# Moving band loads to the sync queue, storing k once and re-timing a planned macaron block on one core

## The reference

```
x = x + 0.5 * ffn(layernorm(x))        # 8 experts, summed: (silu(x @ wg) * (x @ wu)) @ wd, 128 -> 512 -> 128
x = x + attention(layernorm(x))        # 16 heads of 8 features, causal, with rotary positions
x = x + 0.5 * ffn(layernorm(x))        # the same weights
```

## Time and profile before

| | us |
|---|---|
| median of 3 runs | 1333.13 |
| lowest, highest | 1331.54, 1337.11 |
| the profiled execution | 1328.16 |
| its span, first to last instruction | 1326.4 |
| PE busy | 1307.4 |
| DVE, ACT, POOL busy | 1212.7, 1062.8, 1061.4 |

### The profile page before, as it was taken

One profiled execution on the slowest core, in us unless ns is written; L12 is line 12 of the kernel. 1 busy time (PEld: TensorE's weight loads), 2 busy tenths in 40 slices (PEclk: granted clock), 3 DMA queues, 4 the chain that ended last, 5 costly groups with the idle time before them and its releaser, 6 DMA issues. The chain is left out here.

```text
span 1326.4 us, 28468 instructions
## 1 busy us (share of the span) xinstructions
PE 1307.4 (99%) x8334; PEld 1051.4 (79%) x8334; DVE 1212.7 (91%) x2611; ACT 1062.8 (80%) x2099; POOL 1061.4 (80%) x979
## 2 busy tenths in 40 slices
PE   8999999999999999999999999999999999999998
PEld 6888888787778787778888778887888778888787
DVE  6887999999999999999999999999999999998665
ACT  6866888878888888888888888887888888887565
POOL 7976888879878887797787878788778887878565
PEclk9999999999999999999999999999999999999999
DMA  6503899999999999999999999999999999997100
GB/s 190 163 1 118 160 217 228 201 224 229 215 222 215 199 197 194 243 196 202 200 209 208 216 206 200 197 227 205 198 206 198 206 219 206 204 188 138 23 5 8
DMA packets 718555, 241.39 MB, mean 182 GB/s; under 512 B 652480, under 2 KB 681920, under 8 KB 718400
## 3 DMA queue, kind: packets, MB, share of 16 engines
q1 hardware_dynamic: 562240, 180.84, 68.0%
q10 hardware_dynamic: 156160, 58.74, 22.4%
HBM read 77.33 MB, written 69.86 MB: 111 GB/s over the span
## 5 line engine op out<-in xcount | busy, mean ns | idle before, releaser
L1247 POOL TENSOR_TENSOR hid_lo<-hid,hid_hi 128x512 fp32r<-128x512 f32 x511 | 658.8, 1297 | 174.2 <-ACT hid_hi L948 92.7
L942 ACT ACTIVATE hid<-work 128x512 f32<-128x512 f32 x512 | 306.2, 600 | 100.9 <-PE work L798 72.0
L948 ACT CAST hid_hi<-hid 128x512 fp32r<-128x512 f32 x512 | 316.2, 625 | 88.2 <-PE acc L814 55.4
L1073 DVE SCALAR_TENSOR_TENSOR hid<-hid,work 128x512 f32<-128x512 f32 x512 | 343.9, 679 | 44.3 <-ACT hid L942 43.7
L1079 DVE TENSOR_TENSOR hid<-hid,work 128x512 f32<-128x512 f32 x512 | 346.3, 680 | 23.8 <-PE work L732 20.5
L1262 POOL TENSOR_TENSOR probs<-exps,probs 128x512 f16<-128x512 f32 (+1 forms) x288 | 304.1, 1061 | 62.0 <-ACT probs L1004 58.9
L1181 DVE TENSOR_REDUCE negmax<-work 128x1 f32<-128x384 f32 (+3 forms) x352 | 219.5, 632 | 0.5
L993 ACT ACTIVATE exps<-work,negmax_shifted 128x512 f32<-128x512 f32 (+2 forms) x320 | 187.6, 601 | 37.6 <-DVE negmax_shifted L1187 27.1
L821 PE MATMUL acc<-hid_lo,wd 128*128 128x512 f32 x512 | 207.2, 409 | 1.2 <-POOL hid_lo L1247 1.1
L730 PE MATMUL work<-xt,wu 128*128 128x512 f32 x512 | 205.1, 401 | 3.0 <-DVE rope L1163 1.3
L813 PE MATMUL acc<-hid_hi,wd 128*128 128x512 f32 x512 | 203.0, 396 | 1.5 <-ACT xn L959 0.7
(11 more groups left out here) (100 smaller groups left out, 1735.0 us busy)
## 6 DMA issues: line engine op xcount, KB each, us to landing
rel_win<-rel_window_scratch ACTq DMA_DIRECT2D x128, 320.0 KB, 3.8
prob_window_scratch<-probs SPq DMA_DIRECT2D x384, 80.0 KB, 3.2
q_scratch<-rope SPq DMA_DIRECT2D x16, 512.0 KB, 4.0
qq<-q_scratch ACTq DMA_DIRECT2D x32, 256.0 KB, 3.6
k_scratch<-rope SPq DMA_DIRECT2D x16, 512.0 KB, 4.8
rel_window_scratch<-g_s SPq DMA_DIRECT2D x32, 256.0 KB, 3.3
k_pad<-k_scratch SPq DMA_DIRECT2D x128, 64.0 KB, 3.5
prob_window_scratch<-probs SPq DMA_DIRECT2D x32, 256.0 KB, 4.0
```

The costliest lines, as they stand in the source:

```text
L942: act.activation(hid[:, arg % HB, :], work[bank_of["gate", arg]][:, :], ACT.Tanh, scale=0.5).then_inc(s_tanh, 1)
L948: act.copy(hid_hi[:, arg % HH, :], hid[:, arg % HB, :]).then_inc(s_hhi, 1)
L1073: dve.scalar_tensor_tensor(out=hid[:, arg % HB, :], in0=hid[:, arg % HB, :], scalar=1.0, in1=work[bank_of["gate", arg]][:, :], op0=ALU.add ...
L1247: pool.tensor_tensor(hid_lo[:, arg % HH, :], hid[:, arg % HB, :], hid_hi[:, arg % HH, :].bitcast(F32), ALU.subtract).then_inc(s_hlo, 1)
```

## The change

Four edits. (1) `LATER` has a number for each tile of queries for the steps of a task and for the loads of windows and bands, and all its numbers are others. (2) `load_band` is a step of SP. (3) k's scratch holds each of its two parts once, and `load_k` reads each row twice by a stride of 0; the rows of q and k are ordered by head and then by feature, so the host's weights and tables are laid out accordingly, and each store moves one part of 128 rows: four stores for q, two for k. (4) Of the first norm ACT scales tiles 0 and 1, DVE tiles 2 and 3, and PE transposes 0, 2, 1, 3.

```diff
-    LATER = {"acc": -978.2, "attention_sum": -208.7, "band_turn": -699.6, "band_values": -929.8, "constants":
+    LATER = {"acc": -771.6, "attention_sum": -130.6, "band_turn": -648.8, "band_values": -988.2, "constants":
...
+    OF_TASK = ("scores", "near", "largest", "shift", "exp", "p_hi", "p_lo", "p_lent", "p_turn", "store_band")
+    def group_of(name, arg):
+        if name in OF_TASK:
+            return name + str(TASKS[arg % NK][1])
+        if name in ("load_window", "load_band"):
+            return name + str(arg % NT)
+        return name
...
-            step("SP", 1.3, at, "qk_store", (t, i), ("qk_lo", (t, i)),
+            step("SP", (2.0, 1.0)[i], at, "qk_store", (t, i), ("qk_lo", (t, i)),
...
-                step("ACT", 0.4, due[last_of(last)] + 5, "load_band", len(BANDS) * gg + u, ("store_band", last_of(last)),
+                step("SP", 0.5, due[last_of(last)] + 5, "load_band", len(BANDS) * gg + u, ("store_band", last_of(last)),
...
-    k_h = nc.dram_tensor("k_scratch", [VB * 4 * P * L], F32, kind="Internal")
+    k_h = nc.dram_tensor("k_scratch", [VB * 2 * P * L], F32, kind="Internal")
...
-                    base = t % VB * 4 * P * L
-                    for copy in range(2):
-                        sp.dma_start(bass.AP((q_t, k_t)[i], base + copy * (1 + i) * P * L,
-                                             [[L, P], [(2 - i) * P * L, 2], [1, L]]),
-                                     rope[:, :, :]).then_inc(s_qst[i], 16)
+                    places = 4 - 2 * i
+                    for place in range(places):
+                        sp.dma_start(bass.AP((q_t, k_t)[i], t % VB * places * P * L + place * H * L,
+                                             [[L, H], [places * H * L, DH], [1, L]]),
+                                     rope[:, place % 2, :]).then_inc(s_qst[i], 16)
...
-                                     bass.AP(k_t, t % VB * 4 * P * L + g * L + a * HG * L,
-                                             [[H * L, 4 * DH], [1, L]])).then_inc(s_kld[arg % 2], 16)
+                                     bass.AP(k_t, t % VB * 2 * P * L + g * L + a * HG * L,
+                                             [[H * L, 2 * DH], [0, 2], [1, L]])).then_inc(s_kld[arg % 2], 16)
+                if name == "load_band":
+                    gg, tiles = arg // len(BANDS), BANDS[arg % len(BANDS)]
+                    top, n = NT * gg + tiles[0], len(tiles)
+                    for k in range(first_of(top), last_of(NT * gg + tiles[-1]) + 1):
+                        sp.wait_ge(*stored(k))
+                    wait(sp, s_bt, 16 * gg)
+                    sp.dma_start(bands[:, tiles[0]:tiles[-1] + 1, :, :, :].rearrange("p i h a r -> p (i h a) r"),
...
-            norm_turned(0, work[2])
+            for n, i in enumerate((0, 2, 1, 3)):
+                pe.wait_ge(*((s_xn, 2 * (i + 1)) if i < 2 else (s_xn_first, i - 1)))
+                done = pe.transpose(work[2][:, i * P:(i + 1) * P], xn[:, i * P:(i + 1) * P], ident[:, :])
+            done.then_inc(s_xnt, 1)
...
-            norm_scaled(0, x_s[0], 0)
+            act.wait_ge(s_shift, 1)
+            for i in range(2):
+                act.activation(xn[:, i * P:(i + 1) * P], x_s[0][:, i * P:(i + 1) * P], ACT.Identity,
+                               scale=rstd[:, i:i + 1], bias=shift[:, i:i + 1]).then_inc(s_xn, 2)
...
-                if name == "load_band":
...
             norm_stats(0, x_s[0])
+            dve.wait_ge(s_shift, 1)
+            for i in range(2, NT):
+                dve.tensor_scalar(xn[:, i * P:(i + 1) * P], x_s[0][:, i * P:(i + 1) * P], rstd[:, i:i + 1],
+                                  shift[:, i:i + 1], ALU.mult, ALU.add).then_inc(s_xn_first, 1)
             norm_lo(0, xt[0], work[2])
```

More of the change, by code:

```diff
@@ new lines, in macaron_kernel @@
+    LATER = {"acc": -771.6, "attention_sum": -130.6, "band_turn": -648.8, "band_values": -988.2, "constants":
[3 rows of a table added]
+             1058.6, "ln_scaled": 26.7, "ln_stats": -1429.2, "ln_turned": -216.7, "lo": -320.2, "load_band0": -1084.5,
[5 rows of a table added]
+             86.1, "prepare_hi": -186.9, "prepare_lo": -372.5, "product": -34.2, "project": -162.4, "project_v": 52.5,
+             "qk_hi": -1105.5, "qk_lo": -783.5, "qk_store": -730.9, "qrel": -58.3, "qrel_copy": -319.3, "qrel_store":
[3 rows of a table added]
+             "store_band3": -349.9, "sum": 605.0, "sum_turned": -704.8, "tanh": -294.5, "up": 31.7, "v_add": 296.5,
+             "v_split": 343.5, "values": -458.6, "zero": 1447.8}
@@ L127, in step @@
             before = [(name, (arg[0], arg[1] - 1) if arg[1] else (arg[0] - 1, PARTS[name] - 1))]
-        steps[name, arg] = (engine, takes, LANDS[engine] if lands is None else lands, time + LATER.get(name, 0.0),
+        steps[name, arg] = (engine, takes, LANDS[engine] if lands is None else lands, time + LATER.get(group_of(name, arg), 0.0),
                             [what for what in after if what[1] is not None],
@@ L492, in macaron_kernel @@
         s_xn = sem("xn_of_tile_ready")
+        s_xn_first = sem("xn_of_first_norm_ready")
         s_xnt = sem("xn_transposed")
@@ L1008, in _ @@
                     t, g = arg // HG, arg % HG
-                    act.wait_ge(s_qst[0], 32 * (t + 1))
+                    act.wait_ge(s_qst[0], 64 * (t + 1))
                     if arg >= 2:
@@ L1143, in _ @@
                     if w == 2:
-                        dve.wait_ge(s_qst[0], 32 * (t + 1))
+                        dve.wait_ge(s_qst[0], 64 * (t + 1))
                     if w == 0:
@@ L1291, with by_heads @@
     f32 = np.float32
-    def dh_major(w):
-        return np.asarray(w).reshape(H, DH, P).transpose(1, 0, 2)
+    def by_heads(w):
+        return np.asarray(w).reshape(H * DH, P)
     def swapped(w):
-        return dh_major(w).reshape(DH // 2, 2, H, P)[:, ::-1].reshape(DH, H, P)
+        return by_heads(w).reshape(H * DH // 2, 2, P)[:, ::-1]
     watt = np.stack([np.asarray(m).reshape(P, P).T for m in (
-        dh_major(inputs["L0_attn_w_q"]), swapped(inputs["L0_attn_w_q"]),
-        dh_major(inputs["L0_attn_w_k"]), swapped(inputs["L0_attn_w_k"]), inputs["L0_attn_w_v"])], axis=1)
+        by_heads(inputs["L0_attn_w_q"]), swapped(inputs["L0_attn_w_q"]),
+        by_heads(inputs["L0_attn_w_k"]), swapped(inputs["L0_attn_w_k"]), inputs["L0_attn_w_v"])], axis=1)
     rel_g, rel_g0 = np.zeros((HQ, 4, DH, R, HQ), rel.dtype), np.zeros((HQ, 4, DH, R, HQ), rel.dtype)
@@ L1321 @@
     window = np.repeat(np.where(w > i + R, 1e30, 0.0), HQ, axis=1)
-    lanes = np.repeat([[0.0, 1.0], [1.0, -1.0], [0.0, 1.0], [1.0, -1.0]], DH * HQ, axis=0)
+    lanes = np.tile(np.repeat([[0.0, 1.0], [1.0, -1.0]], 2 * HQ, axis=0), (DH, 1))
     arrays = {
@@ L1326 @@
         "watt": watt.reshape(P, -1), "wo": wo.reshape(P, -1),
-        "rel_g": rel_g.transpose(1, 2, 0, 3, 4).reshape(P, P),
-        "rel_g0": rel_g0.transpose(1, 2, 0, 3, 4).reshape(P, P),
+        "rel_g": rel_g.transpose(2, 1, 0, 3, 4).reshape(P, P),
+        "rel_g0": rel_g0.transpose(2, 1, 0, 3, 4).reshape(P, P),
         "rel_c": rel_c.reshape(P, -1), "rel_c0": rel_c0.reshape(P, -1),
-        "rel_k0": np.repeat(rel[0], H)[:, None], "rel_v0": np.tile(rel[0], (P, H)),
-        "cos": np.repeat(cos, H, axis=0).astype(f32), "sin": np.repeat(sin, H, axis=0).astype(f32),
+        "rel_k0": np.tile(rel[0], H)[:, None], "rel_v0": np.tile(rel[0], (P, H)),
+        "cos": np.tile(cos, (H, 1)).astype(f32), "sin": np.tile(sin, (H, 1)).astype(f32),
         "window": window.astype(f32), "ident": np.eye(P, dtype=f32), "lanes": lanes.astype(f32),
```

2 lines of the change are left out of this document (added), and 11 rows, old and new, of the table LATER.

## The result

The changed kernel takes 1382.97 us (median of 4 runs, 1381.12 to 1384.32), the kernel before, run beside it, 1335.12 us (4 runs, 1331.54 to 1338.03). The ratio is 1.0373, 95% interval 1.0351 to 1.0395: 3.7% slower, some 48 us. The forecast of 1331, its range of 1325 to 1341 and its verdict of "no change" were all wrong.

What follows compares the result with a forecast made beforehand. TensorE, busy 1307.4 of 1326.4 us, was taken as the bound. Start -0.65, tail -0.4, ACT's relief -1 and k once -0.3 summed to -2.3 us off the 1333.13 median: 1331 us, range 1325 to 1341.

Steps and rivals of the forecast that it cites:

- load_band to SP: 128 band-load issues, 50 us, move from ACT's queue to SP's; SP's lateness counted as 0, bounds 0 to +18 us.
- The sign that I had named: In SP's queue: its waits for POOL's lower halves were to get smaller by some 50 us.
- my 4 to 16: TensorE's idle time in the middle, forecast 8 to 11 us; outside 4 to 16 us the prediction called itself wrong.
- half-speed stretch: Matmuls from 10.97 to about 14 us, 0.43 us apart, at 1.2 GHz: counted 0, bounds -1.6 to 0, far end +1.6.
- Rival B: SP becomes late in the attention stretch, TensorE waits at `values` and `band_values`: 1350 us, or 1341 in half the groups; chance 0.17.
- Arbitration between queue rows: Band loads in SP's row stand behind transposes: landing perhaps 0.2 us later, 4.9 us at the slowest transpose landing.
- Rival B's other sign: Larger DMA landing times, named beside TensorE waits in tens for turned probabilities or bands; no size given.
- ACT's relief: Band-load issues leaving ACT's queue end some of TensorE's waits for ACT: -1 us, bounds -3 to 0.
- The start: First norm scaled by ACT and DVE: first 512-column matmul near 8.7, not 9.39 us; -0.65 us, bounds -0.8 to 0.
- The tail: A down moves ahead of the program's last `up`, so two TensorE waits should go: -0.4 us, bounds -0.6 to +0.4.
- k once: k stored once: 4 MB less DMA traffic, 16 more issues on SP; together -0.3 us, bounds -1.5 to +1.
- due times: New order of gate, up, down and tasks: value 0; floor all 10.34 us of the middle gone, ceiling the same again.

Runs made afterwards that it cites:

- the kernels with 86%: Includes the kernel before with each DMA transpose replaced by two plain copies and band loads issued by SP: SP issuing 86% of 1050 us, time 1353.6 us.
- the stand-ins: Kernels with each DMA transpose replaced by plain copies (two in the main pair), the reciprocal by a multiplication: kernel before 1328.09 us, changed kernel 1359.2 us.

## Why the prediction was wrong, point by point

- **load_band to SP, the step that failed.** "so on the average there is room", and then "I count 0, bounds 0 to +18". The room was there, and more than I saw: one wait row gave 2.2 us a group, while SP's queue issues 862 of 1050 us, some 188 us free. But an average says nothing of a queue in order whose work comes in bursts (four k loads in 2.48 us, single issues of nearly 4) and whose consumers are at most four tasks behind. At 82%, in the kernel before, the bursts were absorbed; in the kernels with 86% they were not. By the stand-ins this edit costs +25.5 us in the kernel before and +39 in the changed one. The sign that I had named came: SP's waits for POOL's lower halves fell from 142.2 to 91.4 us (three lines each, 150 to 1200 us), by the 50 us forecast. I took that for room used up harmlessly, and it wasn't. TensorE's idle time in the middle became 50.6 us, far outside my 4 to 16.
- **The duration was taken from a queue with gaps.** 0.39 us is the row of ACT, where most band loads stand alone; in SP's stream, right behind other issues, the same load takes 0.52. 50 us were 67.
- **The number of those who wait was too small.** I let transposes feed `values` alone and named the buffers in half a sentence without a price. ACT's casts lost 51.1 us more than before (63.9 - 12.8), and behind them stand all other work of ACT, DVE's and TensorE's. Of TensorE's idle time 24.1 us is the direct wait; that much of the rest came this way round is argued from these waits and shown whole for one stall.
- **The clock was left out.** I had priced the half-speed stretch at the start only. New idle times brought six more: an estimated 10 of the 12.6 us by which TensorE's busy time grew.
- **Rival B** had the mechanism (SP late, waits at `values`, 0.17), but its price was the wait of before, 0.57 us, times 32 groups, +18. Measured is a mean of 24.1 / 16 = 1.5 us and up to 5.9 for the direct wait alone. A wait that the old trace shows is one in a queue that keeps up; it can't price a queue that doesn't. The sign of lateness that I quoted, transposes that took 3.9 us to issue, should have weighed more.
- **Arbitration between queue rows.** The Trainium skill (DMA: Bandwidth & Descriptors, "Queues, rings and completion order") says that each DMA engine takes turns between the queue rows. From that I had worked out that band loads would land later behind transposes. The trace doesn't show it: 3.3 us in the median from SP, 3.8 from ACT; only the longest grew, 5.8 to 8.8.
- **Rival B's other sign,** larger landing times, didn't come in the medians either.
- **ACT's relief, -1:** nothing shows it. A gain of that size can't be seen inside the loss, and the kernel before with its band loads on SP had the same relief of ACT and was 25.5 us slower.
- **The start, -0.65:** wrong. The first matmul on 512 columns stands at 9.70, not near 8.7. It starts 2.92 us behind the first scaling (6.78 to 9.70), before 2.79 (6.60 to 9.39). The rows of the changed kernel:

```profile
6.78 1.62 DVE L1092 TENSOR_SCALAR xn<-x,rstd,shift 128x128 f32<-128x128 f32 x2 [1.78 <-POOL shift L1263]
6.88 0.87 ACT L963 ACTIVATE xn<-x,shift,rstd 128x128 f32<-128x128 f32 x2
7.05 1.27 POOL L1253 TENSOR_TENSOR wg<-probs_t,wg 128x512 fp32r<-128x512 f32 x1 [0.30 <-ACT wg L949]
...
8.97 0.59 ACT L967 CAST xt<-work 128x512 fp32r<-128x512 f32 x1 [0.71 <-PE work L807]
...
9.70 0.77 PE L823 MATMUL work<-xt,wg 128*128 128x512 f32 x1 [0.77 <-POOL wu L1253]
```

DVE's two tiles took 1.62 us together, not 2 x 0.22 nor 2 x 0.41: its instruction of 128x128 was 0.35 us once and 1.36 the other time, while POOL worked beside it. The last transpose waited for it, and ACT's gain was lost. In three stand-ins with the same edit the two took 1.52 to 1.55 us. The same step alone was worth nothing in its run.
- **The half-speed stretch, 0:** right. Matmuls still start 0.43 us apart behind the first one, until 12.8 us. The clock column has 1.00 there, so it is the spacing that tells it, not the column.
- **The tail, -0.4:** the two waits of the earlier trace rows are gone; the kernel's last stage idles 3.64 us where 3.75 were, so right in kind and, in total, nearly nothing.
- **k once, -0.3, and due times, 0:** right within what can be told when each is alone (+0.4 and +0.2 us as stand-ins). Yet the order isn't indifferent: two plans of the same work, issued by the same engines, lay 17 us apart, and the three parts together cost 9 us that none costs alone. A sum of single steps can't see this.
- **Still open:** the stand-ins show 31 of 48 us. Issues of over 2 us are frequent only in the originals (from 150 to 1200 us 42 transposes in each, 110 us together in each; in the stand-ins five issues at most); that a queue with such issues is hurt more by added ones is likely but was not shown.

## What to carry to other kernels

An engine that only issues DMAs is a resource like any other: sum its issues over a stretch before giving it more, with durations of issues that stand as closely as the new ones will. Don't measure its room by an average, but ask how many tasks ahead of their consumers the buffers let it be, and what is the longest run of issues in a row. And follow the buffers backwards: the first to stand may be the engine that writes the next task's data, with all its other work behind it.

## What the runs showed of the hardware

- The same band load took 0.378 us to issue on ACT when it stood alone and 0.567 right behind another issue, on SP, nearly always right behind one, 0.521; k's loads took 0.61 on ACT and 0.59 on SP. A transfer of 512 bytes in 64 pieces took 0.62 (row L737), more than a band load of 64 KB: here issuing had a price of its own, whatever the size. The Trainium skill (DMA: Bandwidth & Descriptors, "Issuing engines are not separate DMA queues") calls the issuing engine's own time usually small beside the transfer; here such an issue, 0.62 us, is small beside its landing (2.9 us), and yet 128 of them cost 30 us.
- In the kernel with three copies for each transpose the DMA engines were not the limit: the packets of SP's queue took 50.0% of them, against 68.0% in the kernel before, and it was 150 us slower. For the changed kernel this isn't shown so plainly; its DMA share in the attention stretch is 1.02 against 1.07 before.
- The six stretches of lower granted clock between 150 and 1200 us (0.66 to 0.83 over 5 or 10 us each) all come with a wait of TensorE of 1.5 us or more, but seven other waits of 1.3 to 2.7 us brought none. What the clock cost is an estimated 10 us, against 40.3 us of added idle time.
